# Slot map of a mixture-of-experts layer moved from GpSimd to VectorE, with constants and loads in other places

## The chip, the cores and the metric

One core of a Trainium2 chip runs the whole program. The metric is the device time of one execution in microseconds; lower is better.

## The reference, cut to what matters

x is 4 batches of 1024 tokens of 256 numbers, f32. The result is x plus an attention layer plus an expert layer, both of the normalized x:

```python
xn = layernorm(x)
q, k, v = split(xn @ w_qkv.T)          # 16 heads, q and k in two halves of 8
o = a1 - lam * a2                      # a1, a2: softmax attention of each half, all 1024 keys
attn = rms_norm(o) * 0.2 @ w_proj.T + b_proj
# experts: E = 8, T = 4096 tokens, C = 2*T//E = 1024 slots each
idx1, idx2 = the two largest logits of xn @ wg        # per token
loc = place of the token among those that chose the same expert (cumulative sums of the masks)
keep = loc < C;  slot = idx * C + min(loc, C - 1)
disp[slot] += token * keep             # 8 x 1024 rows
eo = gelu(disp @ w_gate[e]) @ w_down[e]
out = g1 * keep1 * eo[slot1] + g2 * keep2 * eo[slot2]
```

Attention and experts do not depend on each other, so the program may interleave them. The two meet in the sum.

## The kernel before

The program is written by hand, engine by engine, and every order is the order of the code: SP issues the DMAs of the hardware queue, POOL the indirect ones, ACT, DVE and PE have one list each. Semaphores tie the lists together. There is no scheduler.

**Stage 1, normalizing and v.** DVE normalizes x in four groups of eight tiles of 128 tokens (`normalize`, L844), PE transposes it (L1136) and multiplies by the weights of v and of the router in one product per tile (L1125, 128x264), ACT copies v into `v_stage` and the router's logits out (`copy_v`, L710). `v_stage` holds two of four batches. So tile 16, the first of batch 2, may be copied only when batch 0 has been stored: `act.wait_ge(v_out[b % 2], 16 * (b // 2))`, L714. SP stores each batch of normalized tokens to `token_rows` and each batch of v to `v_heads` (L390, L393).

**Stage 2, sixteen q/k units and the slot map.** A unit makes 128 rows of q or k for one batch. PE multiplies (L1181, 3.5 us at full clock) into a pair of PSUM banks, ACT writes the first bf16 part (L747), DVE the f32 rest (L902), ACT the second part (L752), DVE the third (L909), SP stores all three (L441). Three part buffers go round, so ACT's first part of unit n waits for the store of unit n - 3; PE's unit n waits for the rest of unit n - 2.

Beside the units the router's slot map is made. DVE picks two experts per token (`choose`, L873); behind unit 1 (`COUNT_AT`) PE counts earlier tokens and DVE works out slots (`find_slots`, L912). A slot number is a tile of 128 slots and a place in it. To turn slots into token numbers, PE multiplies a one-hot matrix of places (`low_side`, one 128x128 block for each of the 2 x 32 choices and token tiles) with a matrix of tiles (`tile_side`), whose entries are token numbers split in two parts, tile base and lane; 64 products add up in one bank (`map_slots`, L1155, behind unit 11). POOL writes 40 of the 64 blocks of `low_side`, one comparison each (L558), DVE the rest in three instructions (L934) and all of `tile_side` (L939, L944, L949). DVE reads the token numbers (`find_tokens`, L952), POOL fetches 512 token rows at a time with four indirect DMAs (`find_rows`, L538), PE transposes them (`turn_rows`, L1164, the first behind unit 14, `ROWS_AT`), ACT and DVE split them into high and low parts (L740, L961).

The first expert's weights are split too: the high parts by ACT (gate, L761) and POOL (down, L566), the low parts by POOL (L550). SP's list in this stage also holds the loads of v and of q and k of heads 0 to 3 for the next stages (L415, L405), six DMAs behind each store from unit 4 on.

**Stage 3, sixteen expert steps**, two per expert, 512 slots each. PE does eight gate blocks `f` (six matmuls of 512 columns, L1251), the transposes of the next rows, then eight down blocks (twelve matmuls of 256 columns, L1271). ACT applies Gelu and makes the high part of the hidden rows (L772, L774), DVE the low part (L1041). Between blocks PE visits attention: it makes the scores whose row maxima attention needs, eight per step, in two pairs of banks, two at each visit (`smax`, L1193, L1202); DVE reduces each (L1012, 1024 columns). There are four visits per step, behind gate blocks 1 and 4 and down blocks 3 and 6. The down results stay in banks 6 and 7, and DVE copies them out at the end of the step (L1060). At the end of a step ACT and DVE split the next expert's weights (L767, L1033), which SP loads.

**Stage 4, attention** of 64 heads: PE makes transposed scores (L1220), ACT exponentiates (L804), PE multiplies by v (L1232).

## Time and profile before

| | us |
|---|---|
| median of 3 runs | 1784.26 |
| lowest, highest | 1782.41, 2266.64 |
| the profiled execution's own time | 1785.46 |
| its span, first to last instruction | 1783.7 |
| mean granted TensorE clock | 0.992 |

| engine | busy us | share |
|---|---|---|
| PE (TensorE matmul) | 1709.6 | 96% |
| DVE (VectorE) | 1477.1 | 83% |
| ACT (ScalarE) | 1395.5 | 78% |
| POOL (GpSimd) | 608.0 | 34% |

Times in the views count from the span's start. The clock is a share of 2.4 GHz: 1.00 is the upper level, 0.50 the lower (1.2 GHz), and a value between is a mean over a stretch. A matmul's duration includes its way through the array, so a group of matmuls takes less than their durations added up. A row such as "L558 x40" is forty instructions of line 558.

### The profile page before, as it was taken

How to read it: one execution, taken by the hardware profiler on the slowest of the kernel's cores; microseconds unless marked ns; L12 is line 12 of the kernel's file. 1: busy time of each engine (PE TensorE's matmuls, PEld its weight loads, DVE VectorE, ACT ScalarE, POOL GpSimd, SP SyncE). 2: the span in 40 equal slices, each digit the busy share in tenths (PEclk: the TensorE clock that was granted, in tenths of full speed). 3: DMA queues.
4: the chain of work that ended last, by engine and by line, in shares of the span. 5: the costliest groups of instructions: out<-in, count | busy, mean ns of one | idle time of the engine just before them, and what ended most of it. 6: DMA issues, size and time to landing. Idle time of an engine off the chain costs nothing.

```text
span 1783.7 us, 39403 instructions
## 1 busy us (share of the span) xinstructions
PE 1709.6 (96%) x15555; PEld 745.5 (42%) x15555; DVE 1477.1 (83%) x1733; ACT 1395.5 (78%) x2634; POOL 608.0 (34%) x1132
## 2 busy tenths in 40 slices
PE   6868999999999999999999999999999999999999
PEld 5436888888886222222222222222222222222237
DVE  7766777777766999999999999999999999999923
ACT  4534554454453999999999999999999999999993
POOL 1475212222200132433334232335524333442353
PEclk9998999999999999999999999999999999999999
DMA  7554332222202211111111111111111111100003
GB/s 241 197 200 166 101 99 74 68 89 89 83 25 84 61 32 39 29 41 30 38 33 32 39 31 39 29 38 33 35 36 30 40 29 39 32 24 12 14 8 101
DMA packets 92280, 109.66 MB, mean 61 GB/s; under 512 B 17472, under 2 KB 67264, under 8 KB 92096
## 3 DMA queue, kind: packets, MB, share of 16 engines
q1 hardware_dynamic: 85952, 90.36, 16.3%
q0 software_dynamic: 6144, 16.79, 3.3%
q8 instruction: 123, 2.02, 0.5%
q14 instruction: 61, 0.50, 0.1%
HBM read 72.77 MB, written 33.82 MB: 60 GB/s over the span
## 4 chain that ended last, share of the span: by engine, by line
PE 66%; ACT 28%; POOL 3%; DVE 1%; issue 1%; DMA 1%; ACTq 0%; SPq 0%; POOLq 0%; DVEq 0%
ACT arena_t L804 25%; PE banks L1232 19%; PE banks L1220 11%; PE banks L1271 11%; PE banks L1251 10%; PE banks L1202 8%; POOL arena_v L558 2%; PE banks L1291 2%; ACT o_raw L787 2%; PE banks L1125 2%; PE banks L1326 2%; PE banks L1171 1%; PE banks L1181 0%; PE banks L1136 0%; DMA arena_x<-x_in 0%
## 5 line engine op out<-in xcount | busy, mean ns | idle before, releaser
L1012 DVE TENSOR_REDUCE row_half<-banks 128x2 f32<-128x1024 f32 x1024 | 1186.7, 1216 | 132.2 <-PE banks L1202 130.4
L804 ACT ACTIVATE arena_t<-banks 128x512 f32<-128x512 f32 x2048 | 1083.3, 599 | 42.8 <-PE banks L1220 17.5
L1232 PE MATMUL banks<-arena_t,v_ring 128*17 128x256 f32 x8192 | 642.4, 386 | 25.4 <-ACT o_raw L787 25.3
L1232 PEld LDWEIGHTS banks<-arena_t,v_ring 128*17 128x17 f32 x8192 | 136.2, 95 | 408.2 <-issue 240.1
L1220 PE MATMUL banks<-arena_q 50*128 50x512 bf16 x960 | 284.0, 383 | 0.0
L1202 PE MATMUL banks<-arena_q 48*128 48x512 bf16 x960 | 269.7, 384 | 0.0
L1220 PE MATMUL banks<-qk_ring 50*128 50x512 bf16 x896 | 264.0, 385 | 2.7 <-DVE arena_r L1060 2.5
L1202 PE MATMUL banks<-qk_ring 48*128 48x512 bf16 x896 | 250.0, 382 | 0.8 <-DVEq L1005 0.8
L772 ACT ACTIVATE arena_t<-banks 128x512 f32<-128x512 f32 x128 | 76.5, 598 | 207.3 <-PE banks L1251 198.7
L1271 PE MATMUL banks<-w_parts,hidden_parts 128*128 128x256 f32 x1536 | 196.3, 286 | 0.0
L1271 PEld LDWEIGHTS banks<-w_parts,hidden_parts 128*128 128x128 f32 x1536 | 187.1, 192 | 13.6 <-issue 13.6
L1251 PE MATMUL banks<-rows_parts,w_parts 128*128 128x512 f32 x768 | 188.6, 398 | 1.1 <-ACT arena_t L772 1.1
L671 POOL TENSOR_TENSOR neg_parts<-row_neg,ones_bf 128x16 bf16<-128x16 f32 x64 | 16.7, 261 | 449.8 <-DVE row_neg L1019 449.5
L1251 PEld LDWEIGHTS banks<-rows_parts,w_parts 128*128 128x128 f32 x768 | 141.9, 189 | 43.1 <-issue 13.5
L544 POOL DMA_INDIRECT arena_r<-token_rows,token_i x64 | 89.0, 1390 | 178.3 <-PE banks L1171 155.2
L1220 PEld LDWEIGHTS banks<-arena_q 50*128 50x128 bf16 x960 | 63.2, 93 | 202.3 <-ACT arena_t L804 175.0
L581 POOL TENSOR_TENSOR inv_sum<-inv_sum,half_factor 128x16 f32<-128x16 f32 x64 | 13.8, 216 | 384.4 <-DVE inv_sum L1074 384.4
L1220 PEld LDWEIGHTS banks<-qk_ring 50*128 50x128 bf16 x896 | 61.2, 93 | 194.3 <-ACT arena_t L804 165.4
L1041 DVE TENSOR_TENSOR hidden_parts<-arena_t,hidden_parts 128x512 fp32r<-128x512 f32 x128 | 86.1, 687 | 44.4 <-ACT hidden_parts L774 43.7
L774 ACT CAST hidden_parts<-arena_t 128x512 fp32r<-128x512 f32 x128 | 79.4, 621 | 4.1
L621 POOL DMA_INDIRECT gathered<-expert_rows,slot_i x64 | 65.7, 1026 | 10.4 <-issue 5.3
L1181 PE MATMUL banks<-arena_t,w_qk 128*128 128x512 f32 x128 | 59.7, 617 | 7.8 <-DVE rest L902 7.8
(148 smaller groups left out, 1368.1 us busy)
## 6 DMA issues: line engine op xcount, KB each, us to landing
expert_rows<-arena_r SPq DMA_DIRECT2D x16, 512.0 KB, 3.0
q_stack<-arena_q SPq DMA_DIRECT2D x8, 768.0 KB, 5.1
k_stack<-arena_q SPq DMA_DIRECT2D x8, 768.0 KB, 5.0
v_heads<-arena_v SPq DMA_DIRECT2D x4, 1088.0 KB, 5.6
v_ring<-v_heads SPq DMA_DIRECT2D x64, 68.0 KB, 2.9
arena_x<-x_in SPq DMA_DIRECT2D x4, 1024.0 KB, 6.4
token_rows<-arena_x SPq DMA_DIRECT2D x4, 1024.0 KB, 7.8
arena_v<-w_gate_in SPq DMA_DIRECT2D x4, 1024.0 KB, 6.4
```

The costliest lines, as they stand in the source:

```text
L544: nc.gpsimd.indirect_dma_start(out=rows_in[:, s, t, :], out_offset=None, in_=token_rows, in_offset=bass.IndirectOffsetOnAxis(ap=token_i[:, ...
L621: nc.gpsimd.indirect_dma_start(out=gathered[:, t % 2, c, :], out_offset=None, in_=expert_rows, in_offset=bass.IndirectOffsetOnAxis(ap=slot ...
L772: nc.scalar.activation(hidden[:, LO, f, :], banks[:, f % 2, :], ACT.Gelu).then_inc(gelu_done, 1)
L774: nc.scalar.copy(hidden_parts[:, HI, f, :], hidden[:, LO, f, :]).then_inc(hidden_high, 1)
L804: nc.scalar.activation(probs[:, kt % PSLOTS, q, :], banks[:, ST_BANKS[ring_place(i) % 3], :], ACT.Exp).then_inc(exp_done, 1)
L1012: nc.vector.tensor_reduce(halves[:, :, j // 2], banks[:, SMAX_PAIRS[m % 2]:SMAX_PAIRS[m % 2] + 2, :], AX.X, ALU.max, negate=True).then_inc ...
L1041: nc.vector.tensor_tensor(hidden_parts[:, LO, f, :], hidden[:, LO, f, :], hidden_parts[:, HI, f, :].bitcast(F32), ALU.subtract).then_inc(h ...
L1202: mm = pe.matmul(banks[:, SMAX_PAIRS[m % 2] + s, :], heads_qk[g % RING][rows, 0, qt * P:(qt + 1) * P], heads_qk[g % RING][rows, 1, h * CH: ...
L1220: pe.matmul(banks[:, ST_BANKS[place % 3], :], heads_qk[g % RING][rows, 1, kt * P:(kt + 1) * P], heads_qk[g % RING][rows, 0, qh * CH:(qh + ...
L1232: mm = pe.matmul(banks[QUAD * q:QUAD * q + VP, OT_BANK, columns], v_ring[:, g % SLOTS, kt, :], probs[:, kt % PSLOTS, q, columns], start=(k ...
L1251: mm = pe.matmul(banks[:, f % 2, :], gate_parts[e % 2][:, w, c, f * P:(f + 1) * P], rows_parts[:, r, c, :], start=(c == 0 and i == 0), sto ...
L1271: mm = pe.matmul(down, hidden_parts[:, h, f, t * P:(t + 1) * P], down_parts[e % 2][:, w, f, :], start=(f == 0 and i == 0 and t % 2 == 0), ...
```

## The change

1. **Token codes.** Token 128k + p is coded as (128 + p) x 2^k, exact in bf16. A sum with one nonzero term keeps it, and the f32's exponent and upper mantissa bits are the token number plus a constant. So one product column per slot tile replaces two (64 columns in place of 128), and `find_tokens` reads the bank as integers.
2. **Both sides on VectorE.** `low_side` and `tile_side` are laid out with the 64 choice-and-tile indices innermost. DVE makes them in eight tensor_tensor instructions of 2048 elements with all operands bf16, one in each of units 2 to 9, between rest and third part. PE reads both with a stride of 64 elements. POOL's 40 comparisons go.
3. **Constants in xn's place.** The table `numbers` that is compared with lies in the first half of `arena_x`, written by four iotas of POOL once the normalized tokens are stored and transposed; `low_side` lies in the second half.
4. **SP's order in stage 1.** All four stores of token rows and the first gate load stand ahead of the first store of v.
5. **First weights.** ACT makes both high parts, behind units 10 and 11, DVE both low parts behind unit 11, on both sides of `find_tokens`.
6. **Bank pairs and table loads.** The q/k units go round three pairs of banks; PE's unit n waits for the rest of unit n - 3. The exps of the gates move from behind unit 0 to behind unit 12; Gelu's table is loaded behind unit 13. The second half of unit 15 stands behind the second gate block.
7. **Heads 1 to 3** are loaded in expert steps 0 to 2 and later heads follow one by step; only head 0's loads stay in units 5 to 8. v of heads 0 to 3 is loaded in the expert steps, w_down of the first expert behind store 2. The load of expert 1's gate still waits for the last store.
8. **Three visits of maxima:** behind gate block 2 (three), down block 2 (three) and down block 6 (two), on four bank pairs, among them the down banks and the gate banks while these are free.

The diff, cut:

```diff
+        SMAX_PAIRS = (2, 4)
+        EXPERT_SMAX_PAIRS = (2, 4, 6, 2, 4, 0, 2, 4)
...
+            load_gate(0, 0)
+            for b in range(B):
                 sp.wait_ge(v_copied, TB * (b + 1))
                 sp.dma_start(v_heads[b * H:(b + 1) * H]...
-            load_gate(0, 0)
...
-            for i in range(LOW_BY_POOL):
-                c, t = divmod(i, NT)
-                low = nc.gpsimd.tensor_scalar(low_side[:, c, t, :], in_tile[:], slot_low[:, c, t:t + 1], None, ALU.is_equal)
+            for i in range(4):
+                nc.gpsimd.iota(numbers[:, i * P // 4:(i + 1) * P // 4, :], pattern=[[1, P // 4], [0, 2 * NT]], base=i * P // 4,
...
+            def over(ap, rows):
+                return ap[:].rearrange("p c t -> p (c t)").unsqueeze(1).broadcast_to([P, rows, 2 * NT])
+            def low_is(q):
+                rows = slice(q * QUARTER, (q + 1) * QUARTER)
+                nc.vector.tensor_tensor(low_side[:, rows, :], numbers[:, rows, :], over(low_bf, QUARTER),
+                                        ALU.is_equal).then_inc(sides_ready, 1)
...
+            def first_weights_low(which):
+                dve.wait_ge(first_high, which + 1)
+                nc.vector.tensor_tensor(w_parts[0][:, which, LO], w_ring[0][:, which, LO], w_parts[0][:, which, HI].bitcast(F32),
...
             for n in range(4 * B):
                 split_rest(n)
...
+                if n in (COUNT_AT + 1, COUNT_AT + 2):
+                    low_is(n - COUNT_AT - 1)
+                if n in (COUNT_AT + 3, COUNT_AT + 4):
+                    tile_is(n - COUNT_AT - 3)
...
+                if n == MAP_AT:
+                    first_weights_low(0)
+                    find_tokens()
+                    first_weights_low(1)
...
-                mm = pe.matmul(banks[:, MAP_BANK, 0:2 * TILES], low_side[:, c, t, :], tile_side[:, c, t].rearrange("p i n -> p (i n)"),
+                    mm = pe.matmul(banks[:, MAP_BANK, 0:TILES], low_side[:, :, k], tile_side[:, :, k],
...
-                    if f in (1, 4):
-                        for m in range(2):
-                            smax(8 * n + 2 * (f // 4) + m)
+                    if f == 2:
+                        for j in range(3):
+                            expert_smax(n, j)
...
+                    if f == 2:
+                        if n + 1 < 2 * E:
+                            pe.wait_ge(rows_t_ready, 2 * n + 4)
+                        for j in range(3, 6):
+                            expert_smax(n, j)
+                    if f == 6:
+                        for j in range(6, 8):
+                            expert_smax(n, j)
```

On SP at the end of stage 1, the stores of token rows and of v took turns before (arena_x holds the normalized tokens, arena_v the staged v):

```order
L393 DMA v_heads<-arena_v 128x16x136
L390 DMA token_rows<-arena_x 128x8x256
L393 DMA v_heads<-arena_v 128x16x136
L390 DMA token_rows<-arena_x 128x8x256
L393 DMA v_heads<-arena_v 128x16x136
L390 DMA token_rows<-arena_x 128x8x256
L393 DMA v_heads<-arena_v 128x16x136
L385 DMA arena_v<-w_gate_in 128x2x1024
L441 DMA q_stack<-arena_q 128x3x1024 x2
```

and now, at the same place of SP's list:

```order
L398 DMA arena_v<-w_gate_in 128x2x1024
L408 DMA v_heads<-arena_v 128x16x136 x4
L455 DMA q_stack<-arena_q 128x3x1024 x2
L455 DMA k_stack<-arena_q 128x3x1024
L444 DMA arena_v<-w_down_in 128x8x256
L455 DMA k_stack<-arena_q 128x3x1024
```

The four token-row stores stand ahead of the first row of the second piece, so the first v store is now fourth-batch tokens and a gate load later in the queue; w_down comes behind the third store.

On PE, one expert step before (the 12, 18 and 18 matmuls of L1251 are the gate blocks, those of L1271 the down blocks, L1202 the maxima, L1171 the transposes):

```order
L1251 MATMUL banks<-rows_parts,w_parts_54 128x512 x12
L1202 MATMUL banks<-arena_q 128x512 x4
L1251 MATMUL banks<-rows_parts,w_parts_54 128x512 x18
L1202 MATMUL banks<-arena_q 128x512 x4
L1251 MATMUL banks<-rows_parts,w_parts_54 128x512 x18
L1171 MATMUL banks<-ident,arena_r 128x128 x8
L1271 MATMUL banks<-w_parts_54,hidden_parts 128x256 x48
L1202 MATMUL banks<-arena_q 128x512 x4
L1271 MATMUL banks<-w_parts_54,hidden_parts 128x256 x36
L1202 MATMUL banks<-arena_q 128x512 x4
L1271 MATMUL banks<-w_parts_54,hidden_parts 128x256 x12
```

and the same step now:

```order
L1295 MATMUL banks<-rows_parts,w_parts_54 128x512 x18
L1244 MATMUL banks<-arena_q 128x512 x6
L1295 MATMUL banks<-rows_parts,w_parts_54 128x512 x30
L1190 MATMUL banks<-ident,arena_r 128x128 x8
L1317 MATMUL banks<-w_parts_54,hidden_parts 128x256 x36
L1244 MATMUL banks<-arena_q 128x512 x6
L1317 MATMUL banks<-w_parts_54,hidden_parts 128x256 x48
L1244 MATMUL banks<-arena_q 128x512 x4
L1317 MATMUL banks<-w_parts_54,hidden_parts 128x256 x12
```

Six matmuls of maxima stand in one piece twice, four once, and the visit among the down blocks has moved up from behind 48 matmuls to behind 36.

On DVE, units 2 to 4 before, with parts of the tile side between rest (L902) and third part (L909):

```order
L902 SCALAR_TENSOR_TENSOR rest<-banks,arena_q 128x1024
L939 TENSOR_TENSOR arena_r<-tile,slot_tile 128x16x64
L909 TENSOR_TENSOR arena_q<-rest,arena_q 128x1024
L902 SCALAR_TENSOR_TENSOR rest<-banks,arena_q 128x1024
L944 TENSOR_TENSOR arena_r<-arena_r,first_token 128x16x64
L949 TENSOR_SCALAR arena_r<-arena_r,lane 128x16x64
L909 TENSOR_TENSOR arena_q<-rest,arena_q 128x1024
```

and now:

```order
L919 SCALAR_TENSOR_TENSOR rest<-banks,arena_q 128x1024
L965 TENSOR_TENSOR arena_x<-arena_x,low_bf 128x2048
L926 TENSOR_TENSOR arena_q<-rest,arena_q 128x1024
L919 SCALAR_TENSOR_TENSOR rest<-banks,arena_q 128x1024
L965 TENSOR_TENSOR arena_x<-arena_x,low_bf 128x2048
L926 TENSOR_TENSOR arena_q<-rest,arena_q 128x1024
```

Each of these units has one instruction of 2048 elements where it had one or two of 1024.

## Rows read from the trace of the kernel before

**Rows 1.** Busy us by stretch: PE, PEld, DVE, ACT, POOL, clock, DMA share, GB/s.
```profile
300.00:400.00 100.00, 100.00 (x634) 82.48 (x633) 71.57 (x84) 49.41 (x75) 21.71 (x18) 1.00 0.26 83
```
**Rows 2.** The chain of waits, stage 2: start us, us, what.
```profile
69.15 43.16 POOL arena_v L558 x40
...
117.35 3.50 PE banks L1181 x8
...
123.39 0.21 DVE token_i L955
...
136.59 1.97 PE banks L1171 x8
138.56 5.39 PE banks L1181 x8
...
149.29 5.89 PE banks L1251 x18
...
155.72 4.31 PE banks L1251 x18
```
**Rows 3.** Busy us in a stretch with an idle PE, columns as in rows 1.
```profile
130.00:140.00 10.00, 3.41 (x10) 2.44 (x11) 0.89 (x3) 1.41 (x3) 8.60 (x7) 0.60 0.80 298
```
**Rows 4.** Order of time on ACT and DVE, units 13 and 14: start us, us, what.
```profile
124.31 1.02 ACT L747 ACTIVATE arena_q<-banks 128x1024 bf16<-128x1024 f32 x1
...
125.41 1.22 DVE L902 SCALAR_TENSOR_TENSOR rest<-banks,arena_q 128x1024 f32<-128x1024 f32 x1
...
127.75 1.02 ACT L747 ACTIVATE arena_q<-banks 128x1024 bf16<-128x1024 f32 x1
```
**Rows 5.** Groups of instructions, stage 2: busy us, mean ns of one.
```profile
L944 DVE TENSOR_TENSOR arena_r<-arena_r,first_token 128x1024 bf16<-128x1024 bf16 x4 | 4.9, 1218 | 0.0
...
L949 DVE TENSOR_SCALAR arena_r<-arena_r,lane 128x1024 bf16<-128x1024 bf16 x4 | 1.9, 486 | 0.1
```
**Rows 6.** Order of time in stage 1; last two: DMA issues, KB, us to landing.
```profile
33.05 2.67 DVE L849 TENSOR_SCALAR arena_x<-arena_x,mean_var,rstd 128x256 f32<-128x256 f32 x8
...
38.43 0.37 ACT L716 COPY arena_v<-banks 128x256 f32<-128x256 f32 x1 [0.26 <-PE banks L1125]
...
41.77 3.73 PE L1125 MATMUL banks<-w_v_router,arena_t 128*128 128x264 f32 x16
...
v_heads<-arena_v SPq DMA_DIRECT2D x1, 1088.0 KB, 5.8
...
arena_v<-w_gate_in SPq DMA_DIRECT2D x1, 1024.0 KB, 8.7
```
**Rows 7.** The chain at units 0 and 1, and DVE's rest of unit 2.
```profile
61.53 1.28 ACT L755
...
63.45 0.92 ACT arena_q L747
...
70.51 1.21 DVE L902 SCALAR_TENSOR_TENSOR rest<-banks,arena_q 128x1024 f32<-128x1024 f32 x1
```
**Rows 8.** Splitting weights: DVE's low part in step 1; ACT's high part, mean ns.
```profile
191.12 2.28 DVE L1033 TENSOR_TENSOR w_parts<-arena_x,w_parts 128x2048 fp32r<-128x2048 f32 x1
...
L761 ACT CAST w_parts<-arena_v 128x2048 fp32r<-128x2048 f32 x1 | 1.9, 1895 | 0.0
```
**Rows 9.** DMA issues from 123 to 152 us and of expert 1's gate: KB, us to landing.
```profile
k_stack<-arena_q SPq DMA_DIRECT2D x2, 768.0 KB, 3.4
...
arena_x<-w_gate_in SPq DMA_DIRECT2D x1, 1024.0 KB, 5.0
```
**Rows 10.** Expert step 1: chain; a visit in order of time; groups, mean ns.
```profile
187.18 5.75 PE banks L1271 x48
...
193.47 4.51 PE banks L1271 x36
...
202.83 0.61 PE L1202 MATMUL banks<-qk_ring 48*128 48x512 bf16 x4
...
L1202 PE MATMUL banks<-qk_ring 48*128 48x512 bf16 x64 | 9.7, 382 | 0.0
```

More of the change, by code:

```diff
@@ L740, in rows_t_high, with part1 @@
                     nc.scalar.copy(rows_parts[:, HI, c, :], banks[:, rows_bank(n) + c, :]).then_inc(rows_high, 1)
-            for n in range(4 * B):
+            def part1(n):
                 s = n % PARTS
@@ L758, in _ @@
                     nc.scalar.activation(lam_exp[:], lam_sum[:], ACT.Exp).then_inc(exp_out, 1)
-                if n == 4:
-                    act.wait_ge(gate_in[0], 16)
-                    nc.scalar.copy(w_parts[0][:, 0, HI], w_ring[0][:, 0, LO]).then_inc(first_high, 1)
+                if n == GELU_AT:
+                    load_table(ACT.Gelu)
+                if n == HIGH_AT[0]:
+                    first_weights_high(0, gate_in)
+                if n == HIGH_AT[1]:
+                    first_weights_high(1, down_in)
             def next_weights_high(n):
@@ L778, in _ @@
                     rows_t_high(n + 1)
+            load_table(ACT.Exp)
             act.sem_inc(exp_done, len(ST_BANKS))
@@ L928, in find_slots @@
+                link(nc.vector.scalar_tensor_tensor(out=tile_bf[:], in0=slot_tile[:], scalar=1.0, in1=keep[:],
                                                     op0=ALU.add, op1=ALU.mult))
-            HALF_T = NT // 2
-            def low_is(t):
-                tiles = slice(t, t + GROUP)
-                nc.vector.tensor_tensor(low_side[:, 1, tiles, :], in_tile[:].unsqueeze(1).broadcast_to([P, GROUP, P]),
-                                        slot_low[:, 1, tiles].unsqueeze(2).broadcast_to([P, GROUP, P]), ALU.is_equal).then_inc(low_side_ready, 1)
@@ L947, in tile_lanes, with tile_is @@
-            def tile_lanes(c, h):
-                tiles = slice(h * HALF_T, (h + 1) * HALF_T)
-                nc.vector.tensor_scalar(tile_side[:, c, tiles, 1, :], tile_side[:, c, tiles, 1, :], lane[:, 0:1], None,
-                                        ALU.mult).then_inc(tile_side_ready, 1)
+            def over(ap, rows):
+                return ap[:].rearrange("p c t -> p (c t)").unsqueeze(1).broadcast_to([P, rows, 2 * NT])
+            HALF_S, QUARTER = TILES // 2, P // 4
+            def tile_is(h):
+                rows = slice(h * HALF_S, (h + 1) * HALF_S)
+                nc.vector.tensor_tensor(tile_side[:, rows, :], numbers[:, rows.start + 1:rows.stop + 1, :], over(tile_bf, HALF_S),
+                                        ALU.is_equal).then_inc(sides_ready, 1)
@@ new lines, in tile_tokens @@
+            def tile_tokens(h):
+                rows = slice(h * HALF_S, (h + 1) * HALF_S)
+                dve.wait_ge(code_step, 6)
+                dve.wait_ge(sides_ready, 6)
+                nc.vector.tensor_tensor(tile_side[:, rows, :], tile_side[:, rows, :], over(token_code, HALF_S),
+                                        ALU.mult).then_inc(sides_ready, 1)
+            def low_is(q):
+                rows = slice(q * QUARTER, (q + 1) * QUARTER)
+                nc.vector.tensor_tensor(low_side[:, rows, :], numbers[:, rows, :], over(low_bf, QUARTER),
+                                        ALU.is_equal).then_inc(sides_ready, 1)
@@ L1042, in expert_step @@
                                             ALU.subtract).then_inc(hidden_ready, 1)
-                    if f in (0, 3):
-                        for m in range(2):
-                            smax(8 * n + 2 * (f // 3) + m)
+                    if n == 0 and f == 1:
+                        split_low(4 * B - 1)
+                    if f == 1:
+                        for m in range(3):
+                            smax(8 * n + m)
                     if s == 0 and e > 0 and f == 0:
@@ L1053, in expert_step @@
                     next_weights_low(n)
-                for m in range(4, 8):
+                for m in range(3, 8):
                     smax(8 * n + m)
@@ L1146, in count_earlier @@
             def count_earlier():
-                pe.wait_ge(v_copied, NT)
                 pe.wait_ge(mask_ready, 1)
@@ L1155, in map_slots @@
             def map_slots():
[L1156 to L1161 removed]
+                pe.wait_ge(sides_ready, SIDES)
+                for k in range(2 * NT):
+                    mm = pe.matmul(banks[:, MAP_BANK, 0:TILES], low_side[:, :, k], tile_side[:, :, k],
+                                   start=(k == 0), stop=(k == 2 * NT - 1))
                 mm.then_inc(map_psum, 1)
```

203 lines of the change are left out of this document (101 added, 102 removed).

## The prediction

> **What bounds the kernel now.** I read first the busy time by stretch, to see which engine fills which stage, then the chain of waits through the stage that the change touches, then the order of time on single engines inside it. The span has four stages. Up to about 53 us tokens are normalized and v is projected; from there to 149 us come sixteen q/k units and beside them the router's slot map; then sixteen expert steps to 568 us; then attention. In the expert steps PE is busy for 100.00 of 100 us [rows 1]. So a gain in the expert stage must come out of PE's own stream, and attention, which the change leaves alone, just starts earlier or later.
>
> The q/k stage is different: the chain there is not PE. It runs through one POOL group, forty comparisons in 43.16 us, behind which PE's map product starts at 112.3 and gives way to unit 12 at 117.35; then token numbers (ready at 123.60), indirect loads and, at 136.59, the transposes of what they brought, a slow unit 15 at 138.56 (5.39 us), and only from 149.29 a steady PE [rows 2]; the pieces between are Gelu's table load and the handing over between ACT, DVE and PE at the end of unit 15. The reader is to see that in 96 us PE had 16 units of 3.5 us to do. While PE idles its clock falls: in 130 to 140 the granted clock is 0.60, part of it at the 1.2 GHz level [rows 3]. That is why unit 15 takes 5.39 and not 3.50 us, and why the eighteen matmuls at 149.29 take 5.89 where the next eighteen take 4.31 [rows 2].
>
> **The slot map, part by part.** POOL's forty comparisons go, and DVE builds both sides in eight instructions of 2048 elements, one in each of units 2 to 9. A unit without side work cycles like this: ACT's first part at 124.31, DVE's rest at 125.41, then ACT's second part and, behind that, ACT's next first part at 127.75 [rows 4]. The cycle is 3.44 us, call it 3.45, just below PE's 3.5 for a unit. I keep 3.45, since PE now has three bank pairs and runs ahead. In one cycle DVE has two instructions of 1.15 us (1.22 in the row, of which the next instruction overlaps the last 0.07 or so), so 2.3 us, and is free for 1.15.
>
> What do 2048 all-bf16 elements cost with two streams? No row shows it. From above: a product of 1024 with one f32 stream takes 1218 ns [rows 5], 1.15 start to start, so twice as many at most 2.3. From below: the one-stream bf16 operation takes 486 ns for 1024 [rows 5], so about 0.9. I take 1.2. The new instruction has the types of the fast row (no f32 operand at all), but two streams where it has one; half of its rate is 1.0 to 1.2. Then it just fits into the 1.15 that are free and units 2 to 9 cost 8 x 3.45 = 27.6. At 2.3 the unit is 2.3 + 2.2 = 4.5 us and DVE sets it: 8 x 1.05 = 8.4 more.
> The Trainium skill, "VectorE: DVE Perf Modes", the perf-mode tier table, has a 2x form for a tensor_tensor of 16-bit data, 1224 ns for 2048, and 2293 ns at fp32. By it the sum would be the one I take; the 1218 ns row neither shows nor refutes it, as one of its streams is f32.
>
> **A wait that gets longer.** The change also turns SP's order: before, each v store stands behind its own batch of token rows; now all four token-row stores and the first gate load stand ahead of the first v store. ACT may not write tile 16 of v_stage before that store has landed. The fourth batch of token rows is final only with the normalization that runs from 33.05 for 2.67 us, so at 35.7 [rows 6]. Ahead of v store 0 there are then two transfers of 1 MB. Of one alone the row says 5.8 us to landing, of a gate load right behind a v store 8.7 [rows 6]. So two take 8.7 + 0.4 (issue), and each further one 8.7 + 0.4 - 5.8 = 3.3. Three issued from 35.7 on: the third lands at 35.7 + 9.1 + 3.3 = 48.1. ACT began tile 16 at 38.43 in the profile; its v tiles are released to PE two copies later, so PE's tile 20, which started at 41.77 [rows 6], starts at 48.1 + 0.5 = 48.6. PE loses 6.8 us; idle for so long it falls to the 1.2 GHz level and loses more: unit 15 lost 1.9 behind a longer gap and the block at 149.29 1.6 behind shorter ones [rows 2], I take 1.4. Together 8.2 us, and all after it is late by this. From below: if the three transfers ran side by side, v store 0 would land at 36.5 + 5.8 = 42.3 and cost 1 us.
> The Trainium skill, "DMA: Bandwidth & Descriptors", Queues, rings and completion order, has SP's transfers on one ring per DMA engine, consumed in ring order; by that rule they do not run side by side. With the page's 358 GB/s of HBM per core (3.2 MB in 9.0 us) the landing would be near 46.5 and the loss near 6.5.
>
> **The sum up to the experts**, in the profile's time. Unit 2's rest starts on DVE at 70.51 [rows 7]. The exps and their table load, 1.92 us from 61.53 to 63.45 on ACT's part of the chain [rows 7], leave unit 0, so 68.6; plus the late v stage 8.2: 76.8. Units 2 to 9: 27.6, so 104.4. The load of w_down now stands behind store 2 and so ahead of store 3, whose slot ACT needs again for unit 6. It takes 3.3 us, worked out above, and between landing and need there is room for about half: 1.7, so 106.1. Unit 10: 3.45 plus ACT's copy of the gate weights, 1.90 [rows 8]: 111.4. In unit 11 from rest to second subtraction 2.3 + 1.14, then DVE's low half of the gate weights, 2.2 (2.28 for the row of that shape [rows 8]), then two small instructions of 0.4 together (the second is 0.21 [rows 2]): token numbers at 117.5, against 123.60 before. The product for the map (after unit 11, from about 105 on) took 5.0 us [rows 2] and now loads its weights with a stride, which no row prices: between nothing more and twice as much, it ends by 115, with room. Numbers to transposes: 13.0 before (123.60 to 136.59 [rows 2]); with no head loads beside it I take 12.0: 129.5. ACT and DVE reach unit 14 at about 129.5 too: units 12 and 13 carry the exps, the table load for Gelu and the second weight subtraction, three things of about 2 us each. So a faster gather would give nothing, as that is next in line.
> From there the pattern of before: transposes 1.97 and unit 15 at 5.39, cold as before since PE idled some 10 us: 136.9. The first two gate blocks, two thirds of the 4.31 for three [rows 2], 2.8: block 2 starts at 139.7. Gelu's table is there and unit 15's second half comes after two blocks, so nothing stands between. Before, block 2 started at 149.29 and lost 1.58 to the clock (5.89 - 4.31): 150.9. Gain so far 11.2 us.
>
> **Heads 1 to 3 and the rest of SP.** Their twelve loads each leave the units and come beside the experts, where PE doesn't wait for them: head 1 is needed two steps later, some 52 us. One thing is hurt: load_gate(1, 1) still waits for the last store. That comes from unit 15, whose second half is now behind two gate blocks: ready at 143.2, issued at 143.5, landed 3.4 later, and the gate 5.0 behind that [rows 9]: 151.9. ACT wants it when the eighth block is done, at about 150, and copies the rows' high parts only after it (1.9 and 1.1), DVE the low parts by 156; PE wants those after the third down block, 154. Loss 2.0, bounds 0 and 4.
>
> **Three visits.** A visit of two maxima costs PE 0.54 in the chain (187.18 + 5.75 to 193.47), and the blocks behind it take 4.51 for 36 matmuls, where 48 take 5.75, so 36 should take 4.31: 0.20 more. Together 0.74 [rows 10]. The four matmuls stream in two pairs, the second 0.23 behind the first (0.61 for the group less 0.38 for one [rows 10]); two pairs are 0.46, so 0.27 belongs to the visit and not to its maxima. One visit fewer in 16 steps: 16 x 0.27 = 4.3. Bounds 0 (all of it goes with the maxima) and 4.3. I take 4.3 since the 0.20 stands in a block of matmuls that has no maximum in it. What hides DVE's side: it does the same eight reductions, and is busy for 72 of 100 us [rows 1].
>
> Sum: 11.2 - 2.0 + 4.3 = 13.5 us off the profiled execution's own 1785.46 (span 1783.7 and 1.8 around it), so 1772.0; the median of the runs shown is 1.2 below that execution: **1770.8, say 1771 us**.
>
> **Rivals.**
> A: the v store lands early enough (side by side, or from a shorter queue). For it: one store lands 5.8 after issue. Against: two together took 9.1, so they queue. All 8.2 come back: 1763 us.
> B: DVE runs the sides at one element per cycle. For it: 1218 ns for 1024 with bf16 in and out. Units 2 to 9 take 8.4 more, of which the DMA wait of 1.7 is hidden: 1771 + 6.7 = 1778 us.
> C, the other side: slower than before. Place: PE's second visit in each step. It moved from behind the fourth down block to behind the third, where it waits for DVE's low rows. In the profile those end at 191.2, where the weight subtraction behind them starts [rows 8]; the third block ends at 187.18 + 36 x 0.12 = 191.5 [rows 10]. The room is 0.3 us. Each us that DVE's two row subtractions come later costs PE 0.7 to 1 us in 15 steps. Slower than before begins where the loss per step passes 13.5/15 = 0.9 us, so where they end 1.2 us later than now. What could do it is the three reductions in one piece (3.5 us), which push the hidden subtractions back. Against it: five gate blocks follow in which DVE has 1.4 - 0.6 us free each. At 1.5 us a step: 1771 + 22 = 1793.
> D: the saved visit gives nothing, the first step's wait is 4: 1777.
>
> **How the numbers follow.** Forecast 0.50, A 0.15, B 0.18, C 0.06, D 0.11. The forecast alone spans 1766 to 1776. For the range I go down past A's 1763 by its unknown (a gather and a stage without any clock loss, 5 us) to 1758, and up past B and D to 1783, which leaves out C and combinations of B with D. Two per cent, about what a measurement of this kernel can tell from no change, is 35.7 us. Even A, with everything hidden, stays at 21. Faster by more 0.03; slower by more 0.02, the far end of C; within 0.95.
>
> **What would show it.** ACT's copy of v tile 16 waiting for the v_heads DMA until about 48 (A: no gap). The 2048-element comparisons at about 1.2 us, units 3.45 apart. Token numbers near 118, transposes near 130, gate block 2 near 140. Expert steps of 26.0 instead of 26.29 us apart, no PE wait for rows_parts in the visit behind the third down block except in the first step. Attention's 64 heads as long as before. I am wrong if the stage ends elsewhere than 137 to 143 us or if the steps get longer.

## The result and the profile after

The changed kernel takes 1770.18 us in the median, the kernel before, run beside it, 1783.34. The ratio is 0.9925, with a 95% interval of 0.9912 to 0.9938: 13.4 us, or 0.75%, off. The forecast was 1771 us, 13.5 off. The profiled execution took 1769.89 us with a span of 1768.1, 15.6 under the span of before. One of the four executions of each kernel took 2267 us, the changed kernel's at a mean granted clock of 0.655, and one of experiment 6 took 3051 us; the ratios leave these out.

The expert steps first, in the columns of [rows 1]:

```profile
300.00:400.00 100.00, 100.00 (x655) 85.11 (x654) 73.43 (x85) 47.52 (x72) 23.84 (x18) 1.00 0.27 86
```

PE is still full there. The gain must be in the stages ahead of it and in PE's own stream.

The chain of waits of the changed kernel, from v to the first expert step (start us, us, what), which answers [rows 2, 7, 10]:

```profile
37.75 11.69 DMA v_heads<-arena_v
...
50.10 6.55 PE banks L1147 x16
...
79.76 1.14 DVE rest L919
80.90 1.13 DVE arena_x L965
...
106.71 9.49 PE banks L1179 x64
116.19 5.72 PE banks L1202 x8
...
134.16 1.21 DVE rows_parts L978 x2
...
135.61 3.01 PE banks L1295 x12
...
145.59 5.14 DMA arena_x<-w_gate_in
150.75 1.91 ACT w_parts L781
...
154.51 0.82 PE banks L1244 x6
```

POOL's 43.16 us are gone from the chain. A new piece stands at its head, a v store that takes 11.69 us to land, and PE's v tile 20 starts at 50.10 where it started at 41.77 [rows 6]. From then on the stage is late, and it makes that up: the first gate block starts at 135.61, where it was 143.4 before. Unit 11 is followed by a map product of 9.49 us, which is a link of the chain now.

DVE in order of time, units 10 to 12 (start us, us, engine, line, operation; in brackets the idle time before it and what ended it), first the end of the eight side products:

```profile
105.44 1.22 DVE L960 TENSOR_TENSOR arena_r<-arena_r,token_code 128x2048 bf16<-128x2048 bf16 x1
...
107.77 1.22 DVE L919 SCALAR_TENSOR_TENSOR rest<-banks,arena_q 128x1024 f32<-128x1024 f32 x1
...
113.03 1.23 DVE L919 SCALAR_TENSOR_TENSOR rest<-banks,arena_q 128x1024 f32<-128x1024 f32 x1 [1.65 <-ACT arena_q L743]
...
119.00 0.20 DVE L972 TENSOR_SCALAR token_i<-token 128x64 int32<-128x64 f32 x1
...
122.99 1.22 DVE L919 SCALAR_TENSOR_TENSOR rest<-banks,arena_q 128x1024 f32<-128x1024 f32 x1 [1.59 <-ACT arena_q L743]
```

A side product takes 1.22 us. Token numbers are ready at 119.2, against 123.6 in [rows 2]. Unit 12's rest is late, at 122.99: its product stood behind the map product on PE.

### The profile page after: what moved, and what is told of

Its sections match the earlier page's. It is cut to its first block, busy times and chain, and to the rows that moved or that the text cites. A ratio compares the mean times of both kernels' runs of the same rounds, so it can differ in the third digit from the quotient of the medians.

```text
span 1768.1 us, 39365 instructions
## 1 busy us (share of the span) xinstructions
PE 1708.8 (97%) x15555; PEld 753.3 (43%) x15555; DVE 1472.5 (83%) x1728; ACT 1396.8 (79%) x2637; POOL 559.5 (32%) x1095
## 4 chain that ended last, share of the span: by engine, by line
PE 66%; ACT 28%; DVE 3%; DMA 2%; issue 1%; ACTq 0%; SPq 0%; DVEq 0%
ACT arena_t L821 25%; PE banks L1274 19%; PE banks L1262 11%; PE banks L1317 10%; PE banks L1295 10%; PE banks L1244 8%; PE banks L1340 2%; ACT o_raw L804 2%; PE banks L1147 2%; PE banks L1375 2%; DVE rest L919 1%; PE banks L1190 1%; DMA v_heads<-arena_v 1%; PE banks L1179 1%; DMA k_stack<-arena_q 1%
## 5 line engine op out<-in xcount | busy, mean ns | idle before, releaser
L1295 PE MATMUL banks<-rows_parts,w_parts 128*128 128x512 f32 x768 | 182.6, 393 | 2.5 <-DVE rows_parts L978 2.5
L617 POOL DMA_INDIRECT gathered<-expert_rows,slot_i x64 | 65.8, 1028 | 10.3 <-issue 3.7
L624 POOL TENSOR_SCALAR gathered<-gathered,gates 128x256 f32<-128x256 f32 x64 | 58.8, 922 | 0.0
```

The lines of the kernel that those rows point to most:

```text
L617: nc.gpsimd.indirect_dma_start(out=gathered[:, t % 2, c, :], out_offset=None, in_=expert_rows, in_offset=bass.IndirectOffsetOnAxis(ap=slot ...
L1295: mm = pe.matmul(banks[:, f % 2, :], gate_parts[e % 2][:, w, c, f * P:(f + 1) * P], rows_parts[:, r, c, :], start=(c == 0 and i == 0), sto ...
```

## The experiments

Eleven kernels ran, one of them twice. Each gain or loss against the changed kernel is the difference of the two ratios to before, times 1783 us. Each ratio has an interval of 0.0013 to 0.0017 on either side, so a difference of two has some 0.0021, or 3.7 us. Experiments 2, 6 and 7 gained less than that: there the traces have to show what the ratios can't. Spans of single profiled executions stand beside the medians.

The experiments undo or vary the order on SP, the visits and the types of the side products. Parts 5 to 7 of the change, and the move of the comparisons from POOL to DVE itself, were not undone one by one; what they are worth is read from the traces alone.

**1. The order of v and token rows undone.**

```diff
-            load_gate(0, 0)
-            for b in range(B):
                 sp.wait_ge(v_copied, TB * (b + 1))
...
+            load_gate(0, 0)
```

> The changed kernel with one part undone: SP's order of before for the token rows and the v stores (token-row stores b, then v store b, and the first gate load behind all four), everything else as changed. Theory (the late v store is the largest loss of the change): v store 0 lands near 36 us instead of 49.4, ACT's copy of tile 16 no longer waits, PE's v tile 20 starts near 42 instead of 50.1, unit 2's rest on DVE comes near 68.5 instead of 79.7, and the whole is 11 us faster than the changed kernel: about 1759 us, 24 under the kernel before. Rival (that stage has room elsewhere: POOL's token numbers or DVE's first side product become next in line, or the token rows now land too late for the gather): the v wait goes but the rest of unit 10 moves by less than 5 us, total 1764 to 1770.

1760.41 us, ratio 0.9876 (0.9859 to 0.9892): 8.7 us faster than the changed kernel, and the span, 1758.8, is 9.3 shorter. PE in order of time:

```profile
37.06 3.73 PE L1146 MATMUL banks<-w_v_router,arena_t 128*128 128x264 f32 x16
40.62 1.04 PE L1157 MATMUL banks<-ident,arena_x 128*128 128x128 f32 x8
41.49 3.73 PE L1146 MATMUL banks<-w_v_router,arena_t 128*128 128x264 f32 x16
```

No idle time ahead of tile 20 at 41.49, and unit 2's rest comes at 69.35 instead of 79.68. POOL's iotas, for whose sake the token rows might be stored first, are still early enough: they run from 53.93 for 7.86 us, and DVE compares from 70.49 on. 10.3 us are there at unit 2, 9.8 at the first gate block, 9.3 at the end. Another 1.1 us is lost at once, as the iotas now run beside DVE's work on the slots:

```profile
56.62 1.34 DVE L904 CAST mask_bf<-mask 128x128 bf16<-128x128 f32 x1
```

The same cast takes 0.23 in the changed kernel (68.05), where the iotas are over by then. So the stage behind has hardly any slack that would have hidden the late store, and one edit of the change costs two thirds of what the change brings.

**2. Only the gate load behind the v stores**, the token rows still ahead of them.

```diff
-            load_gate(0, 0)
             for b in range(B):
                 sp.wait_ge(v_copied, TB * (b + 1))
...
+            load_gate(0, 0)
```

> The changed kernel with one part undone: the first gate load stands behind the four v stores on SP as before; all four token-row stores still stand ahead of them. Theory (transfers on SP's queue land in order, and each one of 1 MB ahead of v store 0 costs it 3.3 us): v store 0 lands at 46.1 instead of 49.4, PE's v tile 20 starts 3.3 us earlier, and the whole is 3.3 to 4 us faster than the changed kernel. Rival (v store 0 waits for the token rows alone, and the gate load runs beside them): landing stays at 49.4, total stays.

1766.42 us, ratio 0.9905 (0.9888 to 0.9921): 3.6 us faster. Its profiled execution was its fastest, 1763.73, with a span 6.2 shorter. The chain there, and PE behind it:

```profile
37.15 8.12 DMA v_heads<-arena_v
```
```profile
45.94 5.27 PE L1147 MATMUL banks<-w_v_router,arena_t 128*128 128x264 f32 x16 [3.01 <-ACT logits L713]
```

One transfer of 1 MB less in front, and the store lands 8.12 us after its issue instead of 11.69: 3.57, where 3.3 was worked out. PE's block of 16 is shorter too, 5.27 for 6.55: the mean granted clock in it is 0.72 where it was 0.57. Had the three transfers shared the way side by side, taking one out would have brought the store forward as well, so this alone doesn't show a queue. The landings in the changed kernel do (KB, us from issue to landing):

```profile
token_rows<-arena_x SPq DMA_DIRECT2D x1, 1024.0 KB, 5.6
arena_v<-w_gate_in SPq DMA_DIRECT2D x1, 1024.0 KB, 8.3
v_heads<-arena_v SPq DMA_DIRECT2D x1, 1088.0 KB, 11.7
```

They were issued at 36.72, 37.12 and 37.75, and so landed at 42.3, 45.4 and 49.4, one behind the other.

**3. Four visits of maxima again.**

```diff
-        EXPERT_SMAX_PAIRS = (2, 4, 6, 2, 4, 0, 2, 4)
+        EXPERT_SMAX_PAIRS = (2, 4) * 4
...
-                    if f == 2:
-                        for j in range(3):
-                            expert_smax(n, j)
+                    if f in (1, 4):
+                        for m in range(2):
+                            smax(8 * n + 2 * (f // 4) + m)
```

(the same on the down side, at blocks 3 and 6, and on DVE, with the waits that go with the old pairs; visits and bank pairs go back together)

> The changed kernel with one part undone: eight maxima of an expert step in four visits of two, as before, with the pairs of before; everything else as changed. Theory (a visit costs PE 0.27 to 0.31 us of its own): expert steps 26.29 us apart again instead of 25.98, 16 x 0.31 = 4.9 us slower than the changed kernel, about 1775. Rival (the shorter steps come from something else, such as the twelve head loads or the missing waits, and not from the number of visits): steps stay at 25.98 and the total at 1770.

1774.46 us, ratio 0.9954 (0.9938 to 0.9971): 5.2 us slower than the changed kernel. One gate side in the chain of four visits, and the same side of the changed kernel:

```profile
191.07 2.75 PE banks L1293 x12
193.82 0.54 PE banks L1244 x4
194.36 4.31 PE banks L1293 x18
198.67 0.54 PE banks L1244 x4
199.21 4.32 PE banks L1293 x18
```
```profile
189.43 4.11 PE banks L1295 x18
193.53 0.75 PE banks L1244 x6
194.29 7.07 PE banks L1295 x30
```

Both hold 48 gate matmuls, and no wait stands in either: 2.75 + 4.31 + 4.32 = 11.38 with two visits, 4.11 + 7.07 = 11.18 with one. The visit's price in the block behind it is 0.20. The maxima themselves take 0.54 for two and 0.75 for three, so 4 x 0.54 = 2.16 a step become 0.75 + 0.75 + 0.54 = 2.04. Together 0.32 a step; steps stand 26.29 and 25.98 apart.

**4. The small operands of the side products in float32.**

```diff
-        low_bf = sb("low_bf", [P, 2, NT], BF16)
+        low_bf = sb("low_bf", [P, 2, NT], F32)
```

(also `tile_bf` and `token_code`)

> The changed kernel with the two sides of the slot map and the token codes kept as float32; same values, same instructions, same order. PE's product for the map takes float32 operands then. Theory (the 1.22 us of the 2048-element products on DVE rest on all operands being 16-bit; with float32 each takes about 2.3, the bound of the two 1218 ns rows of 1024): units 2 to 9 take 8 x 4.5 = 36 us instead of 28.1, and the whole is 7 to 9 us slower than the changed kernel, plus whatever the map product gains in length: 1777 to 1783. Rival (the type does not matter, the instruction is limited otherwise): 1.22 us each, total 1770.

1775.95 us, ratio 0.9964 (0.9950 to 0.9978): 7.0 us slower. The group of instructions (busy us, mean ns of one; the type named is that of the first operand), of this kernel and of the changed one:

```profile
L965 DVE TENSOR_TENSOR arena_x<-arena_x,low_bf 128x2048 bf16<-128x2048 bf16 x4 | 9.1, 2280 | 0.0
```
```profile
L965 DVE TENSOR_TENSOR arena_x<-arena_x,low_bf 128x2048 bf16<-128x2048 bf16 x4 | 4.9, 1215 | 0.0
```

One float32 stream out of three is enough to go from 1215 to 2280 ns, and units go from 3.47 to 4.47 us apart: from unit 2's rest to unit 10's it is 35.75 us instead of 28.09. The Trainium skill, "VectorE: DVE Perf Modes", the perf-mode tier table, has 1224 ns for 2048 elements of a tensor_tensor with 16-bit data; the trace agrees, with 1215. One phrase of the expectation was wrong: the sides that PE reads stay bf16, only the small operands change, and the map product still takes 9.5 us.

**5. The map product four times**, with and without strides. Three more products into the same bank, overwritten by the true one.

```diff
+                    pe.matmul(banks[:, MAP_BANK, 0:TILES], flat_low[:, k * P:(k + 1) * P], flat_tile[:, k * TILES:(k + 1) * TILES],
+                              start=(k == 0), stop=(k == 2 * NT - 1))
...
+                    pe.matmul(banks[:, MAP_BANK, 0:TILES], flat_low[:, k * P:(k + 1) * P], tile_side[:, :, k],
...
+                    pe.matmul(banks[:, MAP_BANK, 0:TILES], low_side[:, :, k], flat_tile[:, k * TILES:(k + 1) * TILES],
```

> The changed kernel with the map product run four times in a row into the same bank, the last one the true one, so nothing is left out and the first three are overwritten: first both operands contiguous, then contiguous weights with a strided moving side, then strided weights with a contiguous moving side, then both strided as in the changed kernel. 64 products of 64 columns each. Theory (weights read with a stride are what makes the 9.5 us, 149 ns a product, at either clock level): the first and second take 3 to 5 us each (50 to 78 ns a product), the third and fourth 9.5 each. Rival 1 (the moving side's stride): second and fourth 9.5, first and third short. Rival 2 (neither; it is 64 columns or the clock at its 1.2 GHz level): all four alike, or long exactly where the granted clock is 0.50.

1782.99 us, one execution. The chain, in the order of the expectation:

```profile
105.16 2.04 PE banks L1181 x64
107.20 7.11 PE banks L1184 x64
114.32 5.62 PE banks L1187 x64
119.94 9.30 PE banks L1190 x64
```

Contiguous on both sides is 32 ns a product, a strided moving side 111, strided weights 88, both 145. Neither the theory nor one of its rivals holds alone: each stride costs, and the moving one more. The 32 was measured at the upper level alone and the 88 at the lower alone, so how much of the 88 is the clock this run doesn't say. The 111 held at both: 11 products a us at a clock of 1.00 and, behind 112 us, at 0.50. That the clock is not what makes the true product long shows in the changed kernel itself (columns as in [rows 1]):

```profile
106.70:110.30 3.60, 3.59 (x25) 3.60 (x26) 2.47 (x3) 2.11 (x3) 0.00 (x0) 1.00 0.70 260
110.30:116.00 5.70, 5.70 (x42) 5.70 (x41) 2.92 (x3) 4.40 (x4) 0.00 (x0) 0.50 0.51 184
```

25 products in 3.6 us at the upper level, 42 in 5.7 at the lower (those under way at a bound count on both sides of it): nearly the same pace. The Trainium skill, "SBUF — State Buffer", in its section "Door 1: The DMA port swizzle", has it that an engine's access that goes to a new 16-byte line each time pays a penalty, and that a stride is free up to 8 bf16 elements; here the stride is 64 elements, and the trace agrees in direction (32 ns against 145). The three added products took 14.8 us and the span grew by 13.1. That is not room: this execution was 1.5 us ahead at unit 2's rest (78.17 for 79.68), before the edit could act.

**6. The map product behind unit 12.**

```diff
-                if n == MAP_AT:
+                if n == MAP_AT + 1:
                     map_slots()
```

> The changed kernel with one part moved: on PE the map product stands behind unit 12 instead of behind unit 11. Theory (the product of 9.5 us is on the path only because unit 12 stands behind it: ACT waits 4.7 us for that unit): unit 12's rest on DVE no longer waits and comes 1.5 us earlier, the first gate block 1 to 1.5 us earlier, total 1 to 1.5 us faster than the changed kernel. Rival (the token numbers and the gather behind them are next in line, and they now come 3.5 us later): transposes later than 128.6, gate block 0 where it was or later, total from 1770 up to 1773.

1768.35 us, ratio 0.9918 (0.9901 to 0.9934): 1.2 us faster by the medians, which the intervals don't separate from nothing. The same kernel once more, for a trace:

> The changed kernel with the map product behind unit 12, once more, for a trace. Theory: unit 12's rest on DVE comes about 1.3 us earlier than the changed kernel's 122.99 and the first gate block about 1 us earlier than 135.61; total 1768 to 1769. Rival: the gate block starts at the same time or later, and the gain of 1.2 us comes from elsewhere.

1768.36 us, span 1766.6, 1.5 shorter. DVE:

```profile
119.26 0.22 DVE L970 TENSOR_SCALAR token<-banks 128x64 f32<-128x64 int32 x1 [0.18 <-PE banks L1179]
...
121.83 1.22 DVE L919 SCALAR_TENSOR_TENSOR rest<-banks,arena_q 128x1024 f32<-128x1024 f32 x1
```

Unit 12's rest is 1.16 us earlier, the first gate block 0.96 (134.65). The numbers now wait for the map product, but for only 0.18 us, so both rows are as the theory has them. The rival's place was real too: the rows' transposes came at 130.12 instead of 128.60, as PE waited 1.5 us for the gather, and the chain to the first gate block runs through them now and no longer through DVE's rows. So the move gains only what lay between these two chains.

**7. The second gate and down loads earlier.**

```diff
+                    if n == 14:
+                        sp.wait_ge(map_psum, 1)
+                        load_gate(1, 1)
+                        load_down(1, 1)
...
-            sp.wait_ge(map_psum, 1)
-            load_gate(1, 1)
-            load_down(1, 1)
```

> The changed kernel with one part moved: the loads of the second gate block and second down block of the first expert stand behind the store of unit 14 on SP instead of behind that of unit 15. Theory (the first step loses the PE wait of 1.53 us on rows_parts, since ACT has to wait for that gate load): the load lands some 4 to 6 us earlier, ACT does not wait for it, and the whole is 1.5 us faster than the changed kernel, 1768.5. Rival (DVE's low rows are late for another reason, or the load now delays the last stores of q/k units by its own 3 to 5 us): no gain, or up to 3 us slower.

1766.53 us, ratio 0.9911 (0.9894 to 0.9927): 2.5 us faster by the medians, span 3.1 shorter. The chain:

```profile
148.11 4.31 PE banks L1318 x36
152.42 0.76 PE banks L1245 x6
153.17 5.94 PE banks L1318 x48
```

The visit follows its block without a gap, as the theory has it. Of the 3.1 us, 0.56 was there before the edit could act (first gate block at 135.05) and 0.9 came behind the experts, which it doesn't touch; 1.6 belong to it.

**8. All three together.**

> The changed kernel with three edits together: SP's order of before for token rows and v stores, the loads for the second gate and down block of the first expert behind the store of unit 14, and the map product behind unit 12 on PE. Theory (the three act at different places and add up): 9.3 us for the first, as its profiled span is shorter than the changed kernel's, 3.1 for the second likewise, 1 to 1.5 for the third: 13.5 us faster than the changed kernel, about 1756, 26 faster than the kernel before. Rival (the later map product makes the gather late once all else is earlier, or the early gate load delays the last stores): 1758 to 1762.

1761.70 us, ratio 0.9880 (0.9863 to 0.9896). They don't add up: the gate block starts 1.1 us earlier than in experiment 1, at 124.70, and the end is no earlier. So the pairs were run.

> The changed kernel with two edits: SP's order of before for token rows and v stores, and the loads for the second gate and down block of the first expert behind the store of unit 14. The run with all three edits came out at 1761.7 us, no better than the first alone, and lost some 4 us in 150 to 160 us of its trace, where ACT and DVE wait for a release that the profile can't name. Theory (the two edits add up, and it is the moved map product, or the three together, that brings that wait): the wait is not there, 3 us faster than the first edit alone, 1757 to 1758 us. Rival (the early gate load, once the stage is earlier, brings it): wait there, about 1760 to 1762.

> The changed kernel with two edits: SP's order of before for token rows and v stores, and the map product behind unit 12 on PE. Theory A (the moved product alone is worth 1 us here, as in the three-edit run where the first gate block started 1.1 us earlier than with the first edit alone): 1759 to 1759.5 us. Rival B (the moved product brings the unnamed wait of some 3 to 4 us at about 150 to 160 us): 1761 to 1764.

Order and early loads: 1762.12, ratio 0.9876 (0.9860 to 0.9893), the rival's case. Order and unit 12: 1759.36, ratio 0.9860 (0.9843 to 0.9876), theory A's number. Its trace, though, is of its slowest execution (1760.69; the others 1758.39 to 1760.24), with a span of 1758.9, that of experiment 1, and its first gate block is later there (126.8 for 125.8). PE, in order of time:

```profile
120.56 1.95 PE banks L1189 x8
122.52 4.25 PE banks L1201 x8
126.77 2.75 PE banks L1294 x12
```

The rows' transposes wait 2.0 us for the gather, and then they and unit 15 run at the lower level for the most part (clock 0.53 and 0.62 in 120.5 to 124.5). With all three edits they waited 2.3 us and ran at 1.00, in 1.09 and 3.60 us, and the gate block started at 124.70. So whether the moved product gains here hangs on the clock behind that wait, and I read neither gain nor loss into it.

**9. Order, and the gate load alone earlier.** Against the pair above:

```diff
                         load_gate(1, 1)
-                        load_down(1, 1)
...
                 sp.wait_ge(parts_out[s], stored_by(4 * B - 1, s))
+            load_down(1, 1)
```

> The two-edit kernel (SP's order of before, and the loads for the first expert's second gate and down block moved ahead), but only the gate load stands behind the store of unit 14; the down load stands behind the store of unit 15 again. Theory (the earlier start of the steps, without the pause of 1.4 us in the first visit behind a down block, is what brings the wait that the profile can't name): 1761 to 1762 us, and ACT's first Gelu of the second step again some 4.7 us behind PE's start of that step (1.6 in the other traces). Rival (the down load's 1 MB, when it lands early, is what brings it): no such wait, 1757 to 1758 us.

1759.02 us, ratio 0.9859 (0.9842 to 0.9875), 3.1 us under the pair and with ranges that don't touch (1758.52 to 1759.58; 1761.53 to 1762.77), though the intervals of the two ratios do; the span is 3.5 shorter. PE of the pair, then of this kernel, in order of time, with ACT's first Gelu of the second step behind each:

```profile
151.40 2.91 PE L1295 MATMUL banks<-rows_parts,w_parts 128*128 128x512 f32 x12
156.79 2.66 PE L1295 MATMUL banks<-rows_parts,w_parts 128*128 128x512 f32 x6 [2.47 <-ACT arena_t L786]
...
156.14 0.60 ACT L786 ACTIVATE arena_t<-banks 128x512 f32<-128x512 f32 x1 [14.55 <-remote]
```
```profile
151.32 4.27 PE L1295 MATMUL banks<-rows_parts,w_parts 128*128 128x512 f32 x18
155.53 0.82 PE L1244 MATMUL banks<-qk_ring 48*128 48x512 bf16 x6
...
152.92 0.60 ACT L786 ACTIVATE arena_t<-banks 128x512 f32<-128x512 f32 x1 [11.42 <-PE banks L1295]
```

Both steps start at 151.3 to 151.4. In the pair ACT starts 4.7 us behind PE, released by something that the profile can't name ("remote"), and PE then waits for ACT; here it starts 1.6 behind. So it is not the early start that brings the wait (the theory falls); the early down load does, together with the early stage, because in experiment 7 the same load comes as early in the order and there is no such wait. What links a load that was issued at 127 us to a late release at 156 stays open. The edit moves more than that load: in the pair the last q/k store stands behind both loads and lands 6.5 us behind its issue, here 3.4. What waits for it comes later there by about 3 us, the head loads (138.4 for 135.6) and POOL's indirect loads of later rows (the last begins at 153.3, here at 150.7). But in the pair of order and unit 12 the last indirect load begins at 152.3, and there is no such wait, so this is a difference and not a shown cause.

This is the fastest version of the study: 11.8 us under the changed kernel, 25 under the one before.

## Why the prediction was right

It was right in its main mechanisms and near in the sum, and the closeness is partly luck. For the profiled execution it had 13.5 us off and a time of 1772.0; that execution took 1769.89, 15.6 off. The medians, at 13.4 off, are nearer to it than its own terms are, and among the terms errors cancel:

| term | predicted | in the trace |
|---|---|---|
| v store 0 has landed | 48.1 | 49.4 |
| loss of the v stage by it | 6.8 + 1.4 = 8.2 | 8.3 + 3.0 = 11.3 |
| unit 2's rest | 76.8 | 79.7 |
| units 2 to 9 (to rest 10) | 27.6 + 1.7 for a DMA wait | 28.1 in all |
| unit 10 | 5.35 | 5.26 |
| numbers ready, from rest 11 on | 6.1 | 6.2 |
| numbers ready | 117.5 | 119.2 |
| numbers to transposes | 12.0 | 9.4 |
| gate block 2 starts | 139.7 | 138.6 |
| wait in the first down visit | 2.0 | 1.5 |
| three visits, 16 steps | 4.3 | 4.9 |

**The late v store.** Right in kind and confirmed by undoing it: 8.7 us came back. The term that was mis-sized is the clock's, 3.0 us instead of 1.4: v tiles 20 to 23 took 6.55 us where an undisturbed block of 16 takes 3.56. I had taken it from unit 15 and the gate block of before, where only a part of a block ran slow; here nearly a whole one did (mean granted clock 0.57). The landing itself was 1.3 late: 1.0 of it because the first of the three transfers was issued at 36.72 and not at 35.7, the rest in the three, which took 12.7 from there and not 12.4. "Two together took 9.1, so they queue" was no proof, as two that share the way take as long; the three landings of experiment 2 are. The 46.5 in the prediction's sentence on bandwidth does not follow from the figures in it (35.7 + 9.0 is 44.7); no term of the sum rests on it. The Trainium skill, "DMA: Bandwidth & Descriptors", Queues, rings and completion order, has transfers of one ring taken in order; by that rule taking one away brings the next forward by its length, and experiment 2 agrees, with 3.57 us.

**The DMA wait behind unit 2** was priced at 1.7 and is 0.4. Store 3 landed 6.0 us behind its issue instead of the 3.4 of an undisturbed one, so w_down cost it 2.6, not 3.3, and ACT had 2.2 us of room, not 1.6. The late v stage has no part in it: in experiment 1, without it, the store takes 6.0 too, and DVE waits 0.25 there where it waits 0.23 here. This took back part of the v term by chance.

**The side products** at 1.2 us: measured 1.22, and by experiment 4 it is the types that make them so. Rival B was a real rival: with one float32 operand it comes true, and its price of 6.7 is near the 7.0 measured.

**The map product** "ends by 115, with room" was the step that failed outright. It took 9.49 us, just under twice the 5.0 of before, the upper of my bounds, and ended at 116.2; the room was for the token numbers, and for them it held. What I overlooked is unit 12 behind it on PE. ACT waited 4.70 us for that unit; by experiment 6 some 1.2 of it reached unit 12's rest and 1.0 the first gate block.

**The gather** was there by 9.4 us instead of 12.0: PE reached the transposes at 128.60 and did not wait. That the loads of heads 1 to 3 no longer stand beside it is the likely reason, but no run puts them back; where PE did wait for the gather, in experiment 6, it took 10.4. I had written that a faster gather gives nothing, because ACT and DVE are next in line. That held, and more than I meant: the transposes were done early, but unit 14's rest came at 132.94 and not at 129.5 (1.7 late from unit 10, 1.2 from unit 12, the rest from small steps), and the low part of the rows behind it ended at 135.37. That released the first gate block at 135.61. My step had another chain there, a unit 15 at the lower clock, 5.39 us, ending at 136.9. In the trace that unit ran at the upper level in 3.60 us, and it would not have mattered: PE waited 2.5 us behind it for DVE. Two different chains with nearly the same end, and so the term came out right by luck.

**The first step's wait** (1.5 for 2.0), **the visits** (0.31 for 0.27 a step) and **rival C** came out as argued: no visit behind down block 2 waits for DVE's rows in a later step. Experiment 3 excludes rival D. How near DVE's rows are to the point where C would begin was not tried.

So the trace's own sum is 12.3 at gate block 2 (150.9 - 138.6), less 1.5, plus 4.9: 15.7, against the 15.6 by which the span shrank.

## What to carry to other kernels

When a change reorders a DMA queue to feed its new part, price each transfer that now stands ahead of an old one: here a reordering that nobody needed on the path took 8.7 us out of a gain of 22. A layout that makes VectorE fast can make TensorE slow; price both readers, and look at what is queued behind the slower one, not only at who waits for its result. And measure combined edits together: two that gained 8.7 and 2.5 alone gave 8.7 as a pair.

## What the runs showed of the hardware that I had not expected

A matmul of 64 columns costs 32 ns with contiguous operands (at the upper clock level, the only one seen) and 145 to 148 ns when both are read with a stride of 64 bf16 elements, at either level. During that product the granted clock fell to its lower level at 110.3 us though PE's rows show it without a gap, and it stayed there for 10.2 us: 0.50 from 110.3 to 120.5. In the kernel with the order undone and both loads early, ACT's release came 3.2 us and DVE's 1.8 us later (151.68 for 149.90) than in its twin without the early down load, behind PE rows that start at the same time. And iotas of 2048 bf16 elements on POOL take 7.86 us for four (57.66 to 65.5), 1.97 each, done well before DVE first needs them. They are not free for DVE, though: a cast of 128x128 from f32 to bf16 on it takes 0.23 us, and 1.34 to 1.64 in each trace in which it falls beside the iotas (60.06 in the changed kernel with 1.64, 56.62 in experiment 1 with 1.34), while the tensor_tensor instructions beside them keep their length (0.22, at 55.85 in experiment 1).
